# Layer-normed tiles of the projection stage turned through squares by VectorE and DMA instead of by TensorE

## What is computed

```python
x = x + 0.5 * ffn(layernorm(x))     # f1
x = x + attn(layernorm(x))          # projections, attention, output projection
x = x + 0.5 * ffn(layernorm(x))     # f2
# in attn:
q = (h @ Wq)   # 32 heads of 32
k = (h @ Wk)   # 8 heads of 32
v = (h @ Wv)
q = q * cos + rotate_half(q) * sin
k = k * cos + rotate_half(k) * sin
```

## Time and profile before

| | us |
|---|---|
| median of 3 runs (1485.64, 1485.77, 1491.04) | 1485.77 |
| the profiled execution, its own time | 1488.36 |
| its span, from the first to the last instruction | 1486.7 |
| PE busy | 1462.1 (98%) |
| DVE busy | 982.9 (66%) |
| POOL busy | 695.1 (47%) |
| ACT busy | 582.9 (39%) |

### The profile page before, as it was taken

How to read it: one execution, slowest core, us unless ns; L and a number is a source line. 1 busy time by engine, 2 the same in 40 slices (tenths; PEclk the granted TensorE clock), 3 DMA queues, 4 the chain that set the end, 5 groups by cost and what they waited for, 6 DMA issues and landing times. The chain is left out here.

```text
span 1486.7 us, 25706 instructions
## 1 busy us (share of the span) xinstructions
PE 1462.1 (98%) x9000; PEld 1165.2 (78%) x9000; DVE 982.9 (66%) x2753; ACT 582.9 (39%) x1058; POOL 695.1 (47%) x384
## 2 busy tenths in 40 slices
PE   7999999999999999999999999999999999999999
PEld 7999999888888875555555555555489999999988
DVE  6756674647474848898998888889555444444533
ACT  4333333212111136666666666666632211221220
POOL 1322222633343438999999999999602101010101
PEclk9999999999999999999999999999999999999999
DMA  6555554342325271443333444430262423232311
GB/s 244 188 186 193 194 204 163 133 128 99 114 87 149 95 177 41 109 91 80 80 80 80 97 101 105 95 80 23 58 249 71 141 72 118 96 121 92 114 70 71
DMA packets 138164, 174.32 MB, mean 117 GB/s; under 512 B 43056, under 2 KB 93104, under 8 KB 137776
## 3 DMA queue, kind: packets, MB, share of 16 engines
q1 hardware_dynamic: 109744, 149.69, 33.9%
q10 hardware_dynamic: 28304, 23.14, 4.8%
HBM read 109.88 MB, written 67.67 MB: 119 GB/s over the span
## 5 line engine op out<-in xcount | busy, mean ns | idle before, releaser
L1785 ACT ACTIVATE at_probs<-ps 128x512 f32<-128x512 f32 (+1 forms) x640 | 314.9, 560 | 166.8 <-PE ps L1694 162.0
L71 DVE CUSTOM_DVE_ANT_0 ps<-ps,at_score_mask 128x512 f32<-128x512 f32 (+1 forms) x480 | 270.7, 623 | 26.1 <-PE ps L1683 24.2
L401 POOL TENSOR_TENSOR f_x_ring<-f_x_ring,f_half_bias 128x1024 f32<-128x1024 f32 x32 | 76.6, 2395 | 404.1 <-DVE f_low_s L745 404.1
L1626 POOL TENSOR_TENSOR at_added<-at_added,at_probs 128x2048 f32<-128x2048 f32 (+1 forms) x60 | 210.3, 3506 | 2.7 <-ACT at_probs L1785 0.7
L1711 PE MATMUL ps<-at_probs,at_vs 128*32 128x512 f32 (+3 forms) x1536 | 151.0, 496 | 0.3 <-POOL at_probs L1605 0.3
L77 PE MATMUL f_ps<-f_wt_hi,f_hT_hi 128*128 128x400 f32 (+1 forms) x384 | 132.2, 344 | 3.3 <-DVE f_hT_lo L718 3.3
L78 PE MATMUL f_ps<-f_wt_lo,f_hT_hi 128*128 128x400 f32 (+1 forms) x384 | 130.6, 340 | 0.0
L79 PE MATMUL f_ps<-f_wt_hi,f_hT_lo 128*128 128x400 f32 (+1 forms) x384 | 130.6, 340 | 0.0
L77 PE MATMUL ps<-f_wt_hi,f_hT_hi 128*128 128x400 f32 (+1 forms) x384 | 130.2, 339 | 0.0
L78 PE MATMUL ps<-f_wt_lo,f_hT_hi 128*128 128x400 f32 (+1 forms) x384 | 130.1, 339 | 0.0
L79 PE MATMUL ps<-f_wt_hi,f_hT_lo 128*128 128x400 f32 (+1 forms) x384 | 130.0, 339 | 0.0
(11 more groups left out here) (213 smaller groups left out, 3513.5 us busy)
## 6 DMA issues: line engine op xcount, KB each, us to landing
f_x_ring<-in_L_attn_resid SPq DMA_DIRECT2D x16, 512.0 KB, 3.5
x<-f_x_ring SPq DMA_DIRECT2D x16, 512.0 KB, 3.3
early<-x SPq DMA_DIRECT2D x16, 512.0 KB, 3.8
scr_q_hi<-qkv_rope_hi ACTq DMA_DIRECT2D x32, 256.0 KB, 2.0
scr_q_lo<-qkv_rope_lo ACTq DMA_DIRECT2D x32, 256.0 KB, 2.3
scr_ctx<-at_ctxn SPq DMA_DIRECT2D x32, 256.0 KB, 2.7
shared<-scr_ctx SPq DMA_DIRECT2D x16, 512.0 KB, 5.0
f_x_ring<-x SPq DMA_DIRECT2D x16, 512.0 KB, 5.6
```

The costliest lines, as they stand in the source:

```text
L71: return dve.tensor_tensor_reduce(out=src[:, 0:keys], in0=src[:, 0:keys], in1=mask, scale=1.0, scalar=part_max[:, g, own] if c else -3.0e3 ...
L401: pool.tensor_tensor(x_ring[:, u, :], x_ring[:, u, :], half_bias[:], ALU.add).then_inc(bias_added, 1)
L1626: pool.tensor_tensor(added[:, heads, :], first, probs[:, (NU * n + u) % PROBS, heads, :], ALU.add).then_inc(added_done, 1)
L1785: act.activation(probs[:, (NU * n + u) % PROBS, g, cols], score_ps[x % BANKS][:, cols], ACT.Exp, scale=SCALE).then_inc(exp_done, 1)
```

## The change

In the projection stage `turn_h` no longer serves the 12 tiles of chunks 1 to 3; the first four tiles are still turned by TensorE. The others go by squares:

- VectorE writes the normalized tile in the order of squares, and a new `to_blocks` transposes all 32x32 squares of it into `blocks`, the fourth part of `early`.
- SyncE's list gets `turn(t)`: a wait for `in_blocks`, one store of 512 KB with a wait for its landing, and four loads of 128 KB. It stands ahead of the x load of tile t + 2.
- ScalarE's copy to `hT_hi` and VectorE's subtraction to `hT_lo` read `blocks` in SBUF instead of PSUM. They are moved from behind the odd output to the step of the next even output (2, 4, 6, 8). On ScalarE the copy stands behind the square root and ahead of the high part of the rotary sum. On VectorE the subtraction stands behind normalize of the next tile, and `to_blocks` of that tile right behind it, both ahead of the rotary work.

The core of the diff:

```diff
         x_ring = early[:, 0:2, :]
-        h = early[:, 2, :]
+        h, blocks = early[:, 2, :], early[:, 3, :]
         stats = sb("stats", [P, 2, 6], F32)
...
         h_turned = sem("h_turned")
+        in_blocks = sem("in_blocks")
         hT_hi_done = sem("hT_hi_done")
...
+        def landed(t):
+            return TC + 1 + EXCHANGED * (t - TC + 1)
+        def tile_of(part, t):
+            return part[(t // TC) % NCH][:, :, (t % TC) * P:(t % TC + 1) * P]
         k_rows = scr["k_hi"].rearrange("n r t -> (n r) t"), scr["k_lo"].rearrange("n r t -> (n r) t")
...
                 sp.dma_start(x_ring[:, slot, :], x_src[bass.ds(t * P, P), :]).then_inc(x_loaded[slot], 16)
+            def turn(t):
+                sp.wait_ge(in_blocks, t - TC + 1)
+                put_squares(sp, blocks, squares, h_turned, landed(t - 1))
+                get_squares(sp, squares, blocks, h_turned)
...
                 if j in (WRAW + 2, WRAW + 4):
+                    turn(TC + j // 2 - 2)
                     load_x(TC + j // 2, j // 2 % 2)
...
             for t in range(TC + 4, NT):
+                turn(t - 2)
                 load_x(t, t % 2)
+            for t in range(NT - 2, NT):
+                turn(t)
             sp.wait_ge(v_done, (B * NCH - 1) * TC + 1)
...
-            def turn_h(b, t, first_tiles=False):
-                tile = b * (NCH * TC) + t
-                if not first_tiles:
-                    pe.wait_ge(h_ready, tile + 3)
-                    pe.wait_ge(hT_lo_done, tile + 1)
-                hT_ps = turned_ps[t if first_tiles else 0]
-                rows = early[:, t, :] if first_tiles else h
+            def turn_h(t):
                 for c in range(KC):
-                    last = pe.transpose(hT_ps[:, c, :], rows[:, c * P:(c + 1) * P], ident[:])
+                    last = pe.transpose(turned_ps[t][:, c, :], early[:, t, c * P:(c + 1) * P], ident[:])
                 last.then_inc(h_turned, 1)
...
             for t in range(TC):
-                turn_h(0, t, first_tiles=True)
+                turn_h(t)
...
                         last.then_inc(proj_done, 1)
-                    if more and o % 2 == 1 and o // 2 < TC:
-                        turn_h(b, (ch + 1) * TC + o // 2)
                 for s in range(TC):
...
                 tile = b * (NCH * TC) + t
-                act.wait_ge(h_turned, tile + 2)
-                act.activation(hT_hi[(t // TC) % NCH][:, :, (t % TC) * P:(t % TC + 1) * P],
-                               turned_ps[t if early else 0], ACT.Copy).then_inc(hT_hi_done, 1)
+                if early:
+                    act.wait_ge(h_turned, tile + 2)
+                else:
+                    act.wait_ge(h_turned, landed(tile))
+                hi = tile_of(hT_hi, t)
+                if early:
+                    act.activation(hi, turned_ps[t], ACT.Copy).then_inc(hT_hi_done, 1)
+                else:
+                    act.activation(in_squares(hi), squares_of(blocks, KC), ACT.Copy).then_inc(hT_hi_done, 1)
...
                         deviation(b, (ch + 1) * TC + o // 2)
+                    if more and o % 2 == 0 and o:
+                        high_hT(b, (ch + 1) * TC + o // 2 - 1)
                     if o >= 1:
...
                         store_out(b, g - 2)
-                    if more and o % 2 == 1 and o // 2 < TC:
-                        high_hT(b, (ch + 1) * TC + o // 2)
...
                 dve.wait_ge(ln_step, 4 * tile + 5)
-                dve.wait_ge(h_turned, tile + 1)
-                dve.tensor_scalar(h, x_ring[:, t % 2, :], mv[:, 0:1], rstd[:, 0:1], ALU.subtract, ALU.mult).then_inc(h_ready, 1)
+                rows = x_ring[:, t % 2, :].rearrange("p (c b i) -> p c b i", c=KC, i=SQ)
+                dve.tensor_scalar(squares_of(h, KC), rows, mv[:, 0:1], rstd[:, 0:1], ALU.subtract, ALU.mult).then_inc(h_ready, 1)
+            def to_blocks(b, t):
+                tile = b * (NCH * TC) + t
+                if tile == TC:
+                    dve.wait_ge(h_turned, TC + 1)
+                dve.wait_ge(hT_lo_done, tile + 1)
+                wait_apart(dve, h_ready, tile + 3, passed)
+                dve.transpose(blocks, h).then_inc(in_blocks, 1)
             def low_hT(b, t, early=False):
-                hT_ps = turned_ps[t if early else 0]
-                hi, lo = [hT[(t // TC) % NCH][:, :, (t % TC) * P:(t % TC + 1) * P] for hT in (hT_hi, hT_lo)]
+                hi, lo = tile_of(hT_hi, t).bitcast(F32), tile_of(hT_lo, t)
                 dve.wait_ge(hT_hi_done, b * (NCH * TC) + (t + 1))
-                dve.tensor_tensor(lo, hT_ps, hi.bitcast(F32), ALU.subtract).then_inc(hT_lo_done, 1)
+                if early:
+                    dve.tensor_tensor(lo, turned_ps[t], hi, ALU.subtract).then_inc(hT_lo_done, 1)
+                else:
+                    dve.tensor_tensor(in_squares(lo), squares_of(blocks, KC), in_squares(hi), ALU.subtract).then_inc(hT_lo_done, 1)
...
                         normalize(b, (ch + 1) * TC + o // 2)
+                    if more and o % 2 == 0 and o:
+                        low_hT(b, (ch + 1) * TC + o // 2 - 1)
+                    if more and o % 2 == 0 and o // 2 < TC:
+                        to_blocks(b, (ch + 1) * TC + o // 2)
                     dve.wait_ge(proj_done, b * (NCH * NO) + (g + 1))
...
                         rope_sum(b, g - 1)
-                    if more and o % 2 == 1 and o // 2 < TC:
-                        low_hT(b, (ch + 1) * TC + o // 2)
                     if not more:
```

4 lines of the change are left out of this document (2 added, 2 removed).

## The result

The changed kernel takes 1494.22 us (median of 9 runs, 1489.88 to 1496.18) beside 1491.04 for the kernel before on the same chip (9 runs, 1485.64 to 1493.1). The ratio is 1.003, with a 95% interval of 1.0016 to 1.0043: no gain, and a small loss that stays within the 0.5% that the prediction called no change. Over later comparisons the kernel before has medians of 1488.5 to 1488.9, so the 1485.77 from which the prediction started was some 3 us low.

A forecast was written before the change was run, and what follows sets the result against it. TensorE, busy 1462.1 of 1486.7 us, was taken as the bound. 10.5 saved less 0.9 + 0.6 for value waits and 0.5 for GpSimd's port gives 8.5: 1485.77 becomes 1477.3 us, range 1475.0 to 1483.0.

The forecast's parts named there:

- What goes: TensorE in the projections: 12 turns of 0.88 us go, 3.5 us a chunk and 10.5 us in all.
- What VectorE pays: VectorE's pair of outputs goes from 12.58 to 12.0 us; it arrives 2.2 us later a chunk relative to TensorE.
- GpSimd's port: VectorE's low part or normalization held by GpSimd in chunk 0: 0.5 us; as a rival 2.8 more, 1480.1, chance 0.10.
- The DMA round trip: Squares' store and four loads take 6.9 us from the end of `to_blocks`, hidden with 0.5 to spare at output 8.
- the rival with a trip of 7.4 to 8.9 us: Output 8 waits for the squares, above 8.3 each pair does: 1480.0 at 8.3, 1485.4 at 8.9; chance 0.13.
- TensorE's new waits: At value tile 2, for ScalarE's copy: 0.9 us in chunk 1, 0.6 in chunk 0, none in chunk 2.
- I cost both at nothing: SyncE's list: x loads and chunk 0's weight pieces held behind the squares' waits were priced at nothing.
- The slower rival: A trip above 8.9 us paces VectorE's list, gain given back at value tile 2; 1498.0 at 10.3 us, chance 0.06.

The follow-up runs named there:

- e2: The changed kernel without the store of the squares and its four loads, so the squares lie in the wrong places; ratio 0.9971 to the kernel before.
- e5: The changed kernel with ScalarE's high part waiting only for the high part's store and GpSimd's low part for the other; ratio 1.0040 to the kernel before.
- e9: The changed kernel with the last tile's copy behind the high part of sum 7 and its low part behind sum 9; ratio 0.9982 to the kernel before.
- e3: The changed kernel with four PSUM banks instead of two for the value tiles of chunks 0 to 2; 1480.95 us, ratio 0.9953 to the kernel before.
- e6: The changed kernel with four PSUM banks for the value tiles and the waits for the output stores parted; ratio 0.9946 to the kernel before.
- e11: The changed kernel with four value banks and the score mask's load issued ahead of the queries and keys; 1479.4 us, ratio 0.9948 to the kernel before.
- e1: The kernel before with TensorE's 96 transposes left out and the waits around them kept; ratio 0.9979 to the kernel before.
- e10: The changed kernel with the last tile's parts taken late and the output store waits parted, two value banks; 1481.59 us, ratio 0.9961 to the kernel before.
- e7: The changed kernel with ScalarE's copy and VectorE's low part put back behind the odd output; ratio 1.0188 to the kernel before.

## Why the prediction was wrong, point by point

The stage was to be 276.0 us and is 288.0. The 12.0 us are: value waits 8.35 instead of 2.0 (6.35); the lower clock behind two of them (16.73 - 11.28 - 3.71 and 16.48 - 11.39 - 3.35, 1.74 each, and 0.14 in chunk 2: 3.6); the first part, to the values of chunk 0, which gained 2.05 and not 3.5 (1.45); chunk 3, 0.77. Together 12.2, less 0.2 that the outputs of chunks 1 and 2 gained above 3.5.

- **What goes: right.** 3.65 and 3.57 us in chunks 1 and 2, 3.49 in chunk 0 of e2, for 3.5 forecast.
- **What VectorE pays: right in its sum, too low in chunk 0.** Pairs of 11.93 in e2 for 12.0; value waits without transfers 0.54 in chunk 1 (0.9 forecast), none in chunk 2, 1.93 in chunk 0 (0.6 forecast and 0.5 for the port), where three low parts met GpSimd at full price. GpSimd's port was a rival with the right size in e2. In the changed kernel itself the low parts of chunk 0 take 1.2 us again (273.28, 286.68, 299.66), since they come later, behind the copies that wait for the squares; once the normalization is stretched instead, 1.83 us at 284.93.
- **The DMA round trip: the step that failed, in two terms.** "So the transfer is hidden, with 0.5 to spare at output 8" is where it went wrong. Its size was 6.9 us from the rows of f1 and is 8.2 and 8.6 at the last tiles of chunks 0 and 1 and 8.0 in chunk 2. The store (2.6 us) and the issue of the loads up to the last (1.4) are as forecast; the last load lands after 4.5 us at the last tile of chunk 1, where the median of 2.8 was taken. So the rival with a trip of 7.4 to 8.9 us had this right, with its reason, ScalarE's two stores in the same stretch. Traffic as such is no measure: f1 moved 190 GB/s from 120 to 240 us with a median of 2.8, the changed projections 174. What the step left out is the other direction, what the squares do to transfers already there. The prediction named ScalarE's stores as something that could slow the squares, and never asked who waits for those stores. They land 1.0 to 1.1 us later, ScalarE stands 35.7 us for them instead of 7.7, and VectorE's pair grows from 12.0 to 13.3 where the root stands behind one. For chunk 1 a sum of readings closes: 0.9 forecast + 1.2 trip (8.58 - 7.4) + 1.3 pair = 3.4, measured 3.35. It is arithmetic and no experiment: in e5, without the long store waits, the same pair still takes 13.04, since the copy then waits for the squares, and e9, which takes 1.2 us off this wait, moves the low part too.
- **TensorE's new waits: place right, size wrong, and their second price missing.** A wait at value tile 2 that ends with ScalarE's copy was forecast. The granted clock behind it was not in any term, though it is a third of what was lost in the values of chunks 0 and 1 (3.5 of 10.5 us).
- **"I cost both at nothing": right for SyncE's list, and yet 1.45 us are missing in the first part.** 1.19 of them is TensorE's wait at output 8 for the last weight piece. SyncE did not bring it late: it landed at 288.70, 9.4 us before its split. ScalarE rounds it at 296.71, behind the high part of sum 6, and GpSimd splits it behind its own rotary work, stretched by 0.42 us as it begins during a normalization (DVE, then POOL):

```profile
297.88 0.84 DVE L1294 TENSOR_SCALAR early<-early,qkv_mv,qkv_rstd 128x1024 f32<-128x1024 f32 x1
```

```profile
298.12 1.72 POOL L1243 TENSOR_TENSOR qkv_wkv_lo<-qkv_wkv_raw,qkv_wkv_hi 128x512 fp32r<-128x512 f32 x1
```

  It ends at 299.84, and TensorE goes on at 299.89. So what counts is how late the lists of VectorE, ScalarE and GpSimd are, and that the prediction followed to the value tiles alone. The transfers alone don't decide it: e2 has none of them and no wait, but e3, e6 and e11 have them all and wait 0.13, 0.00 and 0.14 us there.
- **Chunk 3: not priced.** TensorE waits 0.88 us for the first head's loads (0.12 before, 1.40 in e1, 0.75 in e2, none in e10). It does not arrive earlier beside them: SyncE issues the first of them 0.3 us after TensorE's last value matmul in every run. They take longer, 12.3 us before and 13.1 after, from the first issue to the landing of the mask; why is not shown. The waits of e3 and e6 are other ones, for ScalarE's last value copy.
- **The slower rival had the right mechanism.** "The gain of TensorE is given back at value tile 2" is what happened, and VectorE's list was paced in part by the transfers. Its deciding point, a trip above 8.9 us, was too high, because it counted only the squares' own trip; and the time it gave, 1498.0, was for trips of 10.3 us, which did not come.

Three things stay open. How the loss is shared between store waits and trip is known only as above: 0.2, 3.5 and 5.7 us of 8.3. A stage is read from one execution, and beside the ratios it is off by up to 3.3 us, both ways, and 4 in e7: -7.2 for e2, where the ratio times 1488.7 gives -4.3, -8.7 and -7.0 for e3, -6.6 and -8.0 for e6. The granted clock over the whole span has a part in that: the profiled execution of the changed kernel has 0.997 and 1489.88 us, its eight other runs 0.991 to 0.994 and 1493.31 to 1496.18; of the kernel before, in the last comparison, runs at 0.999 or above took 1486.1 to 1486.9, those at 0.996 1487.9 to 1489.9. Where those others lose it is in no trace kept here. And why TensorE waits for the last weight piece in some executions with the same transfers and not in others was not tried apart.

## What to carry to other kernels

When a change adds transfers, price them twice: how long their own round trip takes, to its last transfer and among what the other queues issue at that moment, and by how much they delay the transfers that are there, then follow each delayed one to the in-order list that waits for it and to what stands behind in that list. A wait that appears at a pause between two buffers is best cured by buffers: two free PSUM banks brought 7.0 of the 8.5 us forecast by the ratio, while shortening either of two causes that cover each other brought 0.2 or 3.5 of 8.3 us. Buffers only move the place where the late engine is needed next, though: with four banks TensorE stood 2.08 us for ScalarE at the start of chunk 3. And a wait of a few us on TensorE costs more than its length, since the clock behind it has a price too.
